# An eight-layer linear-attention stack followed by cross-attention and a mixture of experts: earlier cross-attention loads, and ScalarE's order within a tile

## What is computed

```python
def attn_stack(x, ...):                       # B = 8 layers, 16 heads of 64, F = 1024
    for i in range(B):
        residual = x
        Q = elu(x @ Wq[i] + bq[i]) + 1
        Kf = elu(x @ Wk[i] + bk[i]) + 1
        V = x @ Wv[i] + bv[i]
        KV, sumK = sum(Kf * V, axis=1), sum(Kf, axis=1)      # over the tokens of a sequence
        att = Q * KV * (1 / (Q * sumK + 1e-6))
        x = layer_norm(gelu(att @ Wo[i] + bo[i]) + residual) * ln1_s[i] + ln1_b[i]
        h = gelu(gelu(x @ W1[i] + b1[i]) @ W2[i] + b2[i])
        x = layer_norm(h + x) * ln2_s[i] + ln2_b[i]
    return x

x = x + attn_stack(layernorm(x), ...)
x = x + cross_attention(layernorm(x), ctx_512, ...)   # 16 heads of 16, softmax
x = x + mixture_of_experts(layernorm(x), ...)         # 8 experts, top 1, and a shared one
```

## Time and profile before

| | us |
|---|---|
| three executions | 3107.61, 3111.68, 3114.46 (median 3111.68) |
| the profiled execution | 3121.35 |
| its span in the profile | 3119.4 |
| first to last X1HI copy (32 tile steps) | 149.7 to 2518.7 |
| start of the cross-attention block | 2560.1 |

### The profile page before, as it was taken

How to read it: one execution, slowest core, us unless ns; L and a number is a source line. 1 busy time by engine, 2 the same in 40 slices (tenths; PEclk the granted TensorE clock), 3 DMA queues, 4 the chain that set the end, 5 groups by cost and what they waited for, 6 DMA issues and landing times. The chain is left out here.

```text
span 3119.4 us, 37809 instructions
## 1 busy us (share of the span) xinstructions
PE 2888.2 (93%) x12878; PEld 2317.2 (74%) x12879; DVE 2397.5 (77%) x3526; ACT 1817.6 (58%) x2732; POOL 885.2 (28%) x590
## 2 busy tenths in 40 slices
PE   5799999999999999999999999999999968997895
PEld 4687888788878887888788778887888756775563
DVE  7779888888888888888988898889888826763111
ACT  4566667576757675767676667666767613441121
POOL 5005221512151215121513151315121233333002
PEclk9899999999999999999999999999999988996997
DMA  3000000010000000100000000000000016000012
GB/s 133 1 1 26 29 18 20 27 29 19 19 27 29 19 20 26 29 19 20 26 29 19 20 26 29 19 20 26 30 19 4 1 50 225 0 0 27 10 44 77
DMA packets 59662, 94.95 MB, mean 30 GB/s; under 512 B 12913, under 2 KB 38769, under 8 KB 57425
## 3 DMA queue, kind: packets, MB, share of 16 engines
q1 hardware_dynamic: 56832, 85.35, 8.4%
q0 software_dynamic: 2640, 7.21, 0.7%
HBM read 82.32 MB, written 10.22 MB: 30 GB/s over the span
## 5 line engine op out<-in xcount | busy, mean ns | idle before, releaser
L333 PE MATMUL PS<-XTHI,WHI 128*128 128x512 f32 x1536 | 625.8, 407 | 51.3 <-DVE EX L633 26.7
L335 PE MATMUL PS<-XTHI,WLO 128*128 128x512 f32 x1536 | 608.4, 396 | 0.0
L334 PE MATMUL PS<-XTLO,WHI 128*128 128x512 f32 x1536 | 605.0, 394 | 0.0
L535 ACT ACTIVATE ATT<-INV,CC,CE 128x128 f32<-128x128 f32 x1024 | 432.0, 484 | 274.4 <-DVE INV L685 165.9
L375 PE MATMUL Y<-W2S,H 128*128 128x256 f32 x2048 | 465.8, 384 | 2.3 <-DVE T L705 1.4
L375 PE MATMUL Y<-WO,ATT 128*128 128x256 f32 x2048 | 454.4, 380 | 5.2 <-ACT ATT L535 5.2
L375 PEld LDWEIGHTS Y<-WO,ATT 128*128 128x128 f32 x2048 | 389.8, 190 | 61.5 <-ACT ATT L535 4.1
L375 PEld LDWEIGHTS Y<-W2S,H 128*128 128x128 f32 x2048 | 391.8, 193 | 58.4 <-DVE T L705 1.8
L258 POOL TENSOR_TENSOR RSTD<-MV,EPS 128x4 f32<-128x4 f32 x68 | 18.6, 274 | 1296.5 <-DVE MV L720 1290.9
L333 PEld LDWEIGHTS PS<-XTHI,WHI 128*128 128x128 f32 x1536 | 292.1, 190 | 119.6 <-issue 43.4
L335 PEld LDWEIGHTS PS<-XTHI,WLO 128*128 128x128 f32 x1536 | 291.8, 190 | 65.2
(11 more groups left out here) (186 smaller groups left out, 4779.2 us busy)
## 6 DMA issues: line engine op xcount, KB each, us to landing
STAGE<-L_attn_Wkvq SPq DMA_DIRECT2D x64, 384.0 KB, 4.0
WO<-L_attn_Wo SPq DMA_DIRECT2D x8, 1024.0 KB, 4.8
W2S<-L_attn_W SPq DMA_DIRECT2D x8, 1024.0 KB, 5.1
STAGE<-L_attn_W SPq DMA_DIRECT2D x32, 256.0 KB, 5.1
WGU<-L_ffn_r_gate SPq DMA_DIRECT2D x8, 512.0 KB, 10.1
WGU<-L_ffn_r_up SPq DMA_DIRECT2D x8, 512.0 KB, 9.4
WD<-L_ffn_r_down SPq DMA_DIRECT2D x8, 512.0 KB, 10.1
rows_in<-ZERO SPq DMA_DIRECT2D x1, 2944.0 KB, 15.5
```

Of the source, the lines that this page charges most:

```text
L333: nc.tensor.matmul(out, whi[:, kc, :], xhi[:, kc, :], start=(kc == 0), stop=False)
L334: nc.tensor.matmul(out, whi[:, kc, :], xlo[:, kc, :], start=False, stop=False)
L335: ins = nc.tensor.matmul(out, wlo[:, kc, :], xhi[:, kc, :], start=False, stop=(kc == KD - 1))
L535: ins = nc.scalar.activation(ATT[:, 2 * p + i, ss], INV[:, b, i, ss], ACT.Identity, scale=CE[:, b, k:k + 1], bias=CC[:, b, k:k + 1])
```

## The change

Three things change.

1. ScalarE, in each slot: the clips and the exponentials of pair 3 are issued ahead of pair 1's `weigh`.
2. ScalarE, in each slot that has an MLP: the gelu table is loaded right behind the X1HI copy, ahead of the XTHI copy, and `gelu_down` of the tile before stands behind the third gelu pass instead of the first.
3. The end of the stack: EX and STAGE are allocated outside of it, and cross-attention's inputs are loaded into them as soon as the last weight split and the last `newton` are done. VectorE does `prepare` for tiles 0 and 1 (eight sequences) and then for tile 2 (four) ahead of its last `slot` of the stack, and GpSimd the two `rstd`; only the last four sequences are prepared within cross-attention. ZN and RO of the mixture lie in EX too.

```diff
@@ class CrossInputs (new)
+    def load(self, sp, x, ctx_in, Wq, bq, Wk, bk, Wv, bv, Wo, bo):
+        sp.dma_start(self.XIN, x.rearrange("b s d -> s b d")).then_inc(self.x_in, 16)
+        sp.dma_start(self.CTXS, ctx_in.rearrange("b s d -> s b d")).then_inc(self.x_in, 16)
...
+    def prepare(self, nc, dve, X, k):
+
+        bs = XPARTS[k]
+        nc.vector.tensor_tensor(X[:, bs, :], X[:, bs, :], self.XIN[:, bs, :], ALU.add).then_inc(self.prep, 1)
...
@@ block.sync
+            sp.wait_ge(w_lo, LAYERS * PIECES)
+            sp.wait_ge(recip, LAST * PAIRS)
+            cross.load(sp, x, *cross_loads)
@@ block.gpsimd
             for t in range(2, TILES + 2):
+                if t == TILES + 1:
+                    for k in range(2):
+                        cross.rstd(nc, pool, HALF, k)
                 slot(LAYERS - 1, t)
@@ block.scalar
-                    if m == 0 and before:
+                    if m == 2 and before:
                         gelu_down(z_b, z_act, g)
...
                     invert(nl, nt, 1)
-                    weigh(nl, nt, 1)
                     clip_keys(nl, nt, 3)
                     clip_queries(nl, nt, 3)
+                    weigh(nl, nt, 1)
                     invert(nl, nt, 2)
                 if tile:
                     act.wait_ge(x1t_mm, g + 1)
                     nc.scalar.copy(X1HI[:, :, :], PS[:, KB:KB + 2, :]).then_inc(x1_hi, 1)
+                    nc.scalar.preload_act_table(ACT.Gelu_apprx_tanh)
@@ block.vector
             for t in range(2, TILES + 2):
+                if t == TILES + 1:
+                    dve.wait_ge(cross.x_in, 32)
+                    for k in range(2):
+
+                        dve.wait_ge(xn, LAST - 2 + k)
+                        cross.prepare(nc, dve, X, k)
                 slot(LAYERS - 1, t)
```

More of the change, by code:

```diff
@@ L64, in attention_stack @@
+def attention_stack(nc, X, ident, cross, cross_loads, x, Wkvq, bkvq, Wo, bo, s1, c1, W1, b1, W2, b2, s2, c2):
     with ExitStack() as ctx:
@@ L76, in attention_stack @@
         W2S = sb("W2S", [P, HC, D])
-        STAGE = sb("STAGE", [P, RING, PIECE])
+        STAGE, EX = cross.STAGE, cross.EX
         BA = sb("BA", [P, 3, HC])
@@ L905, in cross_attention @@
         B = ctx.enter_context(nc.psum_tensor("XB", [P, 512], F32))
[L907 to L912, removed]
+        set0, ones_set, mask_set, kx = (sem(n) for n in ("xset0", "xones_set", "xmask_set", "xkx"))
+        z, mx, sh, rd, o, v1, ob, upd = (sem(n) for n in ("xz", "xmx", "xsh", "xrd", "xo", "xv1", "xob", "xupd"))
         zct_mm, qk_mm, v_mm, s_mm, pt_mm, pv_mm, ot_mm, p_mm = (
@@ L985, in _ @@
             apart(0, 0, 1)
-            rstd(1)
+            cross.rstd(nc, pool, HALF, 2)
             apart(0, 1, 0)
@@ L1104, in run @@
                 weigh(b, j, 1)
-            pe.wait_ge(w_in, 64)
+            pe.wait_ge(cross.w_in, 64)
             pe.wait_ge(ones_set, 1)
@@ L1159, in run @@
                     inputs(b + 2, j)
-            act.wait_ge(bias_in, 64)
+            act.wait_ge(cross.bias_in, 64)
             inputs(0, 0)
@@ L1221, in run, with mixture @@
                 output(b, j, 1)
[L1223 to L1230, removed]
-                ins.then_inc(prep, 1)
-                dve.wait_ge(prep, 3 * k + 2)
-                for b in range(bs.start, bs.stop):
-                    ins = nc.vector.bn_aggr(MV[:, b, :], ST[:, b, :])
-                ins.then_inc(prep, 1)
-            prepare(0)
-            dve.wait_ge(r0, 1)
-            dve.wait_ge(prep, 3)
+            dve.wait_ge(cross.r0, 2)
             normed(0, 0)
             normed(1, 1)
-            prepare(1)
-            dve.wait_ge(bias_in, 64)
+            cross.prepare(nc, dve, X, 2)
+            dve.wait_ge(cross.bias_in, 64)
             values(0, 0)
             shifted(0, 0)
-            dve.wait_ge(r0, 2)
-            dve.wait_ge(prep, 6)
+            dve.wait_ge(cross.r0, 3)
             steps(dve, run)
             update(SEQS - 1)
-def mixture(nc, X, ident, out, ffn):
+def mixture(nc, X, ident, out, cross, ffn):
     with ExitStack() as ctx:
@@ L1257, in mixture, with route @@
         PSX = ctx.enter_context(nc.psum_tensor("PSX", [P, 8, 512], F32))
-        route(nc, X, ident, ffn, EID, ROW, PSX)
+        route(nc, X, ident, cross.rows, ffn, EID, ROW, PSX)
         experts(nc, ident, ffn, EID, PSX)
-        combine(nc, X, ffn.rows_out, ROW, out)
-def route(nc, X, ident, ffn, EID, ROW, PSX):
+        combine(nc, X, cross.rows, ffn.rows_out, ROW, out)
+def route(nc, X, ident, ZN, ffn, EID, ROW, PSX):
     with ExitStack() as ctx:
@@ L1687, in _, with combine @@
             result(PAIRS, 0, False)
-def combine(nc, X, rows_out, ROW, out):
+def combine(nc, X, RO, rows_out, ROW, out):
     with ExitStack() as ctx:
@@ L1739, in decoder @@
             ffn = FeedForward(nc, late)
-            cross_attention(nc, X, ident, ffn, a, a["x"], a["ctx_512"], *(a["L0_xattn_" + n] for n in (
-                "Wq", "bq", "Wk", "bk", "Wv", "bv", "Wo", "bo")))
-            mixture(nc, X, ident, out, ffn)
+            cross_attention(nc, X, ident, cross, ffn, a)
+            mixture(nc, X, ident, out, cross, ffn)
 def packed(a, np):
```

94 lines of the change are left out of this document (51 added, 43 removed).

## The result

| | before | after |
|---|---|---|
| median, us | 3111.26 (3107.61 to 3114.46) | 3060.37 (3059.44 to 3065.93) |
| profiled execution, us | 3121.35 | 3059.44 |
| its span, us | 3119.4 | 3057.6 |

The ratio is 0.9838, with a 95% interval of 0.9823 to 0.9853: faster by 1.6%, some 51 us. The forecast was 3069 with 3059 to 3096.

A forecast was written before the change was run, and what follows sets the result against it. TensorE was taken to bound ordinary slots, VectorE the seven splitting ones. Gains of 25.7 + 9.0 + 0.4 (the table load near tile 30) + 8.0 = 43.1 us gave 3111.7 - 43.1 = 3069 us, range 3059 to 3096.

The forecast's parts named there:

- Ordinary slots: Slots without weight splits, TensorE-bound: both its gelu waits go, 1.14 us in 22 slots and 0.6 in the first, 25.7 us.
- Together 1.14 us a slot: TensorE's losses at chunks 4 and 5 of the MLP product, 0.61 and 0.53 us, waiting for gelu passes 0 and 1.
- The other 23 are of the first kind: Of 30 intervals between X1HI copies, all but seven are slots without weight splits, 75.12 us, bound by TensorE.
- Splitting slots: Seven slots splitting the next layer's projection weights, where VectorE sets the end: ScalarE's chain shortens by 1.29 us each, 9.0 us.
- The rival with up to 7 x 1.8 us more: Splitting slots: up to the whole 3.09 us transposes' wait goes, 12.6 us more, 3056 us; chance .08.
- The table load: ScalarE behind X1HI: the 1.28 us load moves into 4.73 us of idle time and costs nothing; chain 1.29 us shorter.
- The order of the exponentials: Pair 3's exponentials ahead of pair 1's ATT: VectorE did not wait for them, so 0 us gained.
- VectorE takes the 1.14 us back: Rival: no slack at the transposes, ordinary slots stay at 75.1 us, 9.0 + 8.0 are left, 3095 us; chance .14.
- The seam: Stack's end to cross-attention's first copy: +7.6 us for prepare, -15.9 us at block start; 8.0 us gain taken, bounds 5.5 to 9.
- The 2.3 us that the forecast allowed: Cross-attention's start: VectorE normalises beside GpSimd's memsets and masks and can come up to 2.3 us later.
- Slower: Rival: GpSimd's two passes meet VectorE's wide passes, 4 us in each ordinary slot, 45 us slower, 3157 us; chance .06.
- From the profiled execution to the median: The profiled execution stood 9.7 us above the median of the runs shown; the forecast carries this over.

The follow-up runs named there:

- table_load_only: Changed kernel with gelu_down again behind the first gelu pass, the table load still behind X1HI; 3063.97 us, ratio 0.9848 to the kernel before.
- gelu_later_only: Changed kernel without the early table load, gelu_down still behind the third gelu pass; 3093.34 us, ratio 0.9937 to the kernel before.
- second profiles: Kernel before and changed kernel each run once more unaltered; profiled at 3115.51 and 3066.92 us.
- table_back: Changed kernel with both halves of the gelu edit undone, early table load and later gelu_down; 3102.96 us, ratio 0.9969 to the kernel before.
- pass_added: Changed kernel with an unread 128x512 ScalarE copy added behind the last gelu pass of each slot with a tile; 3071.73 us, ratio 0.9868 to before.
- order_back: Changed kernel with pair 1's weigh again ahead of pair 3's clips and exponentials; 3062.49 us, ratio 0.9838 to the kernel before.
- after_again: Changed kernel run once more, unaltered; median 3066.61 us, ratio 0.9848 to the kernel before.

## Why the prediction was right, point by point

- **Ordinary slots, 25.7 us forecast, 32.1 measured.** The direction was right and the load was the right cure, but the sum was 6.4 us short and the reasoning at fault in two steps. The step "Together 1.14 us a slot" took the table load and the place of `gelu_down` as two cures for two waits; table_load_only shows that the load alone removes both, and gelu_later_only that the second edit by itself brings 8 us (half of that in C stages, 8 x 0.52) and nothing beside the load. The step "The other 23 are of the first kind" took one C stage as the pattern of A, B and C. By kind they gave 7 x 1.67 + 7 x 1.45 + 8 x 1.18, and 0.8 for the first: 32.1. The forecast's 1.14 holds for C (1.18). In B the price is the chain's 1.42. In A it is 1.05 at full clock, and the other 0.6 are half-clock stretches: six of the seven A stages of before have one and are longer than 75.8 us (up to 76.96), of after one has (75.66). In the second profiles it was six and two, and in the other traces three to five with the load on the chain and one to four with the load ahead. So the change may have made them rarer, but part of the 0.6 can be the draw of the single execution; this was not tried.
- **Splitting slots, 9.0 forecast.** Measured 7 x 1.38 = 9.7. That the table load is the cause is borne out by table_load_only (81.22) and table_back (82.53). That each of them passes on the chain's 1.29 is not: the first gave 1.98, the other six 1.28 in the mean but only about 0.9 between stages at full clock (82.32 and 82.42 to 81.44), and pass_added shows that in after only the first follows the chain. That the sum came out within 0.7 us is partly luck. The rival with up to 7 x 1.8 us more fell: the transposes still wait, 1.6 to 3.2 us.
- **The table load.** The forecast took 1.29 us, the traces of after show 1.43 between X1HI and the first pass: the load's 1.28, and some 0.15 because a gelu pass may start before the XTHI copy has ended (1677.33, the copy from 1676.41 for 1.02), while the load had waited for its end. The forecast's 1.29 was too small by that. The Trainium skill, ScalarE: Activation LUTs, section What ACT_TABLE_LOAD costs, puts 1380 ns of drain beside the load; the trace does not agree, 0.15 us is all there is here.
- **The order of the exponentials, 0 forecast.** Right (order_back, 0.9838 either way).
- **VectorE takes the 1.14 us back.** This rival had the right observation, no slack at the transposes, and it names what B stages are bound by. It fell because that chain runs through the very ScalarE passes that became earlier; only A kept back some of the 1.42, 0.37.
- **The seam.** End of the stack +7.6 forecast, +7.3 measured (40.79 to 48.12 us from X1HI of tile 31); start of the block -15.9 forecast, -15.7 measured. 8.3 by the sum, 8.0 taken, 8.3 to 8.7 by the traces. The 0.85 us that VectorE loses beside GpSimd's memsets (the XZ pass takes 1.26 us instead of 0.41) was hidden by TensorE's wait for the ones. The 2.3 us that the forecast allowed for it had no row behind it.
- **Slower.** GpSimd's passes met no more of VectorE's than before: the denominators take 3.22 us as in the earlier trace rows, and busy VectorE time per stage is unchanged.
- **From the profiled execution to the median.** To carry the 9.7 us over was sound: the gain was summed from stages of the stack and the seam, and the loop's half-clock iterations, which can make up most of the 9.7 us, were in none of them.

The total: 43.1 forecast, 50.9 by the medians of the first comparison, 48.6 in the pair of second profiles, 45.6 in the rounds of after_again. The median of 3060.4 is inside the range of 3059 to 3096 by 1.4 us only, and outside the forecast's own bounds of 3064 to 3080, which its terms add up to; the range's lower end of 3059 has no term of the sum behind it. That it held is luck as much as foresight. What was forecast too small is 5.6 to 7.1 us in the stack's tiles 0 to 30 (40.3 to 41.8 against 34.7), most of it in A and B stages; the rest is within the scatter between rounds.

## What to carry to other kernels

When two waits follow each other on one chain, cost the first cure and then look at what is left of the second before adding it. Read one stage of every kind that the loop has, and ask for each which engine's delay it would pass on: a single cheap pass added to one engine answered that better than all busy shares. And what is late is worth a look at the idle time ahead of it: a table load, or statistics of a later block, cost nothing in the 4.7 and 14.3 us in which their engines waited anyway, and 1.4 and 7.4 us one instruction later.

## What the runs showed of the hardware

- TensorE's granted clock falls to half for stretches within a loop whose instructions never change, in some executions in seven iterations and in others in one, 1.7 us each, up to 10 us in a run of 3.1 ms. In before the granted clock over the loop was 0.91 in one profile and 0.97 in another.
- A table load between two passes cost 1.42 to 1.43 us, of which 1.28 is the load; passes with no load between them start about 0.1 us before their predecessor's end.
- A ScalarE copy of 128x512 took 0.64 us by itself and lengthened the chain by 0.52.
- A half-clock stretch lengthened iterations of the loop by 1.7 us and A stages of after by 1.0, and S stages, with TensorE's wait at the transposes down from 3.2 to 1.7 us, by nothing (81.4 either way).
- A VectorE pass of 128x256 took 1.26 us beside GpSimd's memset of 128x1024 and 0.41 with GpSimd idle.
